# Weighing x by groups of row tiles in one-core attention with a feed-forward layer, with new orders on every engine

## The reference

```python
q = rope(x @ wq);  k = rope(x @ wk);  v = x @ wv          # one head of 128, float32
s = (q * 128 ** -0.5) @ (k * 128 ** -0.5).T
p = softmax(s - 1e30 * (column > row))                    # causal
x1 = layernorm(x + (p @ v) @ wo)
h = gelu(x1 @ binarized(w1).T + b1)                       # 128 -> 512
y = layernorm(x1 + h @ binarized(w2).T + b2)              # 512 -> 128
```

## Time and profile before

| | us |
|---|---|
| Median of three timed runs (lowest, highest) | 294.69 (294.51, 294.73) |
| The profiled execution | 292.43 |
| Its span in the profile | 290.6 |
| PE busy | 265.5 |
| PEld busy | 234.9 |
| ACT busy | 235.2 |
| DVE busy | 230.8 |
| POOL busy | 165.0 |

### The profile page before, as it was taken

One profiled execution on the slowest core, in us unless ns is written; L12 is line 12 of the kernel. 1 busy time (PEld: TensorE's weight loads), 2 busy tenths in 40 slices (PEclk: granted clock), 3 DMA queues, 4 the chain that ended last, 5 costly groups with the idle time before them and its releaser, 6 DMA issues.

```text
span 290.6 us, 5773 instructions
## 1 busy us (share of the span) xinstructions
PE 265.5 (91%) x1831; PEld 234.9 (81%) x1831; DVE 230.8 (79%) x581; ACT 235.2 (81%) x396; POOL 165.0 (57%) x250
## 2 busy tenths in 40 slices
PE   2779899999979999999999999999999999998760
PEld 2668798998968898889888998998898988896530
DVE  1589989999987996799779976999789457446883
ACT  3185776646599979998899999688999899898892
POOL 2150520561256595639981895269849968888223
PEclk9999999999999999999999999999999999999796
DMA  8951251258649627742586128702663230202205
GB/s 197 200 72 41 52 77 28 62 127 162 134 87 177 175 63 126 174 107 51 94 167 160 26 63 208 178 3 63 194 157 82 59 83 0 76 0 74 71 2 144
DMA packets 58013, 29.22 MB, mean 101 GB/s; under 512 B 33408, under 2 KB 54400, under 8 KB 57984
## 3 DMA queue, kind: packets, MB, share of 16 engines
q1 hardware_dynamic: 57168, 28.07, 43.2%
q10 hardware_dynamic: 816, 0.79, 0.8%
HBM read 9.18 MB, written 4.19 MB: 46 GB/s over the span
## 4 chain that ended last, share of the span: by engine, by line
PE 76%; ACT 10%; DVE 6%; issue 4%; POOL 2%; DMA 2%; SPq 0%; ACTq 0%; POOLq 0%; DVEq 0%
PE bank L561 21%; PE pair L537 16%; PE bank L572 5%; PE bank L621 5%; PE bank L622 5%; PE bank L613 4%; PE pair L590 3%; PE pair L591 3%; PE pair L603 2%; PE pair L605 2%; PE pair L604 2%; PE bank L579 2%; DMA hid<-in_L_attn_wk_dram 2%; ACT hid L987 2%; PE bank L658 2%
## 5 line engine op out<-in xcount | busy, mean ns | idle before, releaser
L359 POOL TENSOR_TENSOR hid_lo<-hid,hid_hi 128x1024 fp32r<-128x1024 f32 x28 | 66.4, 2386 | 25.8 <-ACT hid_hi L994 25.7
L561 PE MATMUL bank<-probT,xa 128*128 128x128 f32 x576 | 69.3, 276 | 0.0
L561 PEld LDWEIGHTS bank<-probT,xa 128*128 128x128 f32 x576 | 66.8, 192 | 0.5
L948 ACT ACTIVATE prob<-pair,negmax 128x128 f32<-128x128 f32 (+3 forms) x64 | 47.4, 741 | 10.6 <-DVE negmax L1399 8.9
L1399 DVE TENSOR_REDUCE negmax<-pair 128x1 f32<-128x128 f32 (+3 forms) x64 | 47.2, 746 | 8.9 <-PE pair L540 8.8
L324 POOL TENSOR_TENSOR tok<-rot_cos,rot_sin 128x512 f32<-128x512 f32 x16 | 20.5, 1281 | 39.4 <-ACT tok L963 39.3
L1409 DVE STREAM_TRANSPOSE turned<-prob 128x128 f32<-128x128 f32 (+7 forms) x56 | 39.1, 719 | 0.0
L537 PE MATMUL pair<-qkT_hi 128*128 128x512 f32 (+2 forms) x96 | 37.5, 391 | 0.3 <-ACT hid L987 0.2
L537 PE MATMUL pair<-qkT_hi,qkT_lo 128*128 128x512 f32 (+2 forms) x96 | 33.3, 347 | 0.0
L537 PE MATMUL pair<-qkT_lo,qkT_hi 128*128 128x512 f32 (+2 forms) x96 | 33.1, 345 | 0.0
L987 ACT ACTIVATE hid<-pair,b_sb,alpha 128x1024 f32<-128x1024 f32 x28 | 33.0, 1208 | 0.1
(11 more groups left out here) (111 smaller groups left out, 638.4 us busy)
## 6 DMA issues: line engine op xcount, KB each, us to landing
probT<-turned SPq DMA_DIRECT2D x96, 104.0 KB, 2.2
probT<-turned SPq DMA_DIRECT2D x128, 40.0 KB, 1.9
xq<-in_L_attn_x_dram SPq DMA_DIRECT2D x28, 128.0 KB, 3.8
xa<-in_L_attn_x_dram SPq DMA_DIRECT2D x7, 512.0 KB, 3.9
out_dram<-res SPq DMA_DIRECT2D x7, 512.0 KB, 3.6
hid<-in_L_ffn_w_dram SPq DMA_DIRECT2D x2, 256.0 KB, 2.9
out_dram<-res SPq DMA_DIRECT2D x2, 256.0 KB, 2.3
xa<-in_L_attn_x_dram ACTq DMA_DIRECT2D x1, 256.0 KB, 3.6
```

The lines of the kernel that those rows point to most:

```text
L359: pool.tensor_tensor(hid_lo[:, j, :], hid[:, j, :], hid_hi[:, j, :].bitcast(F32), ALU.subtract).then_inc(s_hid_lo[j], 1)
L561: ins = pe.matmul(bank_of["px", r // TG, c][:, me], xa[c % 2][:, j, :], probT[g][:, :, spot + j, :], start=j == 0, stop=j == r)
L948: act.activation(prob[r % 3][:, 0:(r + 1) * P], pair_of["score", r, c][:, 0:(r + 1) * P], ACT.Exp, bias=negmax[:, r:r + 1], accum_out=rows ...
```

## The change

Three things are changed.

First, the squares of a group are laid out by column tile j and not by row: square j of row r stands at 4 j + (last row - r). So the squares of all rows of a group with the same j are neighbours, and one product takes up to four of them, 512 columns, with x's tile j as weights. For j beyond the first row of the group only the later rows take part, and the product has 384, 256 or 128 columns. `weigh_group(g, first, last, c)` computes tiles first to last of a group; group 1 is called in two pieces. Group 1 of images 0 and 7 goes on row by row (`weigh_row`). The layout leaves gaps, so a group has 13 and 29 squares, which the carry moves too; POOL sets the gaps to zero at the start. The result's rows stand in reversed order in the bank, and `project_out` reads them so.

Second, score row 4 (640 columns) begins at column 192 of its pair of banks, so it is cut in 320 and 320 columns and not in 512 and 128.

Third, the order of the calls is new on every engine. `x1T_high` on ACT gets a wait for `up` of the image before, since a transpose of x1 can now be issued ahead of an `up`.

The core of the diff; of the orders it shows two lines, and the pieces behind it show the rest.

```diff
-    SPOT = {r: (g, r * (r + 1) // 2 - rows[0] * (rows[0] + 1) // 2) for g, rows in enumerate(GROUPS) for r in rows}
-    SQUARES = [sum(r + 1 for r in rows) for rows in GROUPS]
+    SPOT = {r: (g, rows[-1] - r) for g, rows in enumerate(GROUPS) for r in rows}
+    SQUARES = [TG * rows[-1] + 1 for rows in GROUPS]
...
+        def squares(r, first, last):
+            return slice(SPOT[r][1] + TG * first, SPOT[r][1] + TG * last + 1, TG)
+        def columns(r):
+            first = BANK - (r + 1) * P // 2 if r == TG else 0
+            return first, first + (r + 1) * P
...
             def carry(g, c):
+                if by_squares(GROUPS[g][-1], c) == 1:
+                    sp.wait_ge(s_const, 7 + 4)
                 sp.wait_ge(s_turned[GROUPS[g][-1]], by_squares(GROUPS[g][-1], c))
...
+            for g, rows in enumerate(GROUPS):
+                for j in rows[1:-1]:
+                    pool.memset(turned[g][:, :, TG * j + rows[-1] - j + 1:TG * (j + 1), :], 0.0).then_inc(s_const, 1)
...
-                for lo in range(0, (r + 1) * P, BANK):
-                    hi = min(lo + BANK, (r + 1) * P)
-                    diagonal = hi == (r + 1) * P
+                first, last = columns(r)
+                for lo, hi in ((first, min(last, BANK)), (BANK, last)):
+                    if lo >= hi:
+                        continue
+                    diagonal = hi == last
                     for n, (qp, kp) in enumerate(parts):
-                        ins = pe.matmul(dst[:, lo:hi], qp[:, 0, me], kp[:, 1, lo:hi],
+                        ins = pe.matmul(dst[:, lo:hi], qp[:, 0, me], kp[:, 1, lo - first:hi - first],
                                         start=n == 0, stop=n == 2 and not diagonal)
...
-            def weigh(r, c):
...
+            def weigh_group(g, first, last, c):
+                rows = GROUPS[g]
+                if first == 0:
...
+                    pe.wait_ge(s_probT_in[g], carried(g, c))
+                    next_bank("px", g, c)
+                for j in range(first, last + 1):
+                    n = rows[-1] - max(j, rows[0]) + 1
+                    ins = pe.matmul(bank_of["px", g, c][:, 0:n * P], xa[c % 2][:, j, :],
+                                    probT[g][:, :, TG * j:TG * j + n, :].rearrange("p n m i -> p m n i"),
+                                    start=j == 0, stop=j == rows[-1])
+                if last == rows[-1]:
+                    ins.then_inc(s_px[last], 1)
...
             def x1T_high(h, c):
                 act.wait_ge(s_x1T[h], c + 1)
+                if c > 0:
+                    act.wait_ge(s_up[NF - 1], c)
...
-                scores(7, b - 1)
...
-                weigh(4, b - 3)
+            weigh_group(1, 0, 3, 2)
+            scores(7, 3)
```

More of the change, by code:

```diff
@@ L926, in _ @@
-            opening()
-            for b in range(5, 7):
-                step(b)
-            ending()
+            turn_x0(0)
+            turn_x0(1)
+            project(0, 0)
+            project(1, 0)
+            turn_qk(0, 0)
+            turn_qk(1, 0)
+            turn_qk(2, 0)
+            setup_turn_wv()
+            scores(0, 0)
+            scores(1, 0)
+            scores(2, 0)
+            scores(3, 0)
+            setup_wvo()
+            turn_qk(3, 0)
+            project(0, 1)
@@ new lines, in _ @@
+            project(1, 1)
+            scores(4, 0)
+            scores(5, 0)
+            scores(6, 0)
+            scores(7, 0)
+            turn_row(4, 0)
+            setup_turn_sgn1()
+            setup_turn_sgn2()
+            project(0, 2)
+            turn_row(5, 0)
+            turn_qk(0, 1)
+            turn_qk(1, 1)
+            project(1, 2)
+            weigh_group(0, 0, 3, 0)
+            turn_qk(2, 1)
+            scores(0, 1)
+            turn_qk(3, 1)
+            turn_row(6, 0)
@@ new lines, in _ @@
+            project_out(0, 0)
+            turn_row(7, 0)
+            scores(1, 1)
+            turn_qk(0, 2)
+            scores(2, 1)
+            scores(3, 1)
+            scores(4, 1)
+            scores(5, 1)
+            scores(6, 1)
+            scores(7, 1)
+            weigh_row(4, 0)
+            weigh_row(5, 0)
+            turn_qk(1, 2)
+            weigh_row(6, 0)
+            weigh_row(7, 0)
+            scores(0, 2)
+            scores(1, 2)
+            scores(2, 2)
+            project_out(1, 0)
@@ new lines, in _ @@
+            scores(3, 2)
+            project(0, 3)
+            turn_qk(2, 2)
+            turn_qk(3, 2)
+            project(1, 3)
+            weigh_group(0, 0, 3, 1)
+            turn_x1(0, 0)
+            scores(4, 2)
+            project_out(0, 1)
+            scores(5, 2)
+            scores(6, 2)
+            turn_x1(1, 0)
+            scores(7, 2)
+            weigh_group(1, 0, 3, 1)
+            turn_qk(0, 3)
+            weigh_group(1, 4, 7, 1)
+            up(0, 0)
+            project_out(1, 1)
@@ L947, in exponentials @@
                         act.wait_ge(s_turned[last[0]], by_squares(*last))
-                act.activation(prob[r % 3][:, 0:(r + 1) * P], pair_of["score", r, c][:, 0:(r + 1) * P], ACT.Exp,
+                act.activation(prob[r % 3][:, 0:(r + 1) * P], pair_of["score", r, c][:, slice(*columns(r))], ACT.Exp,
                                bias=negmax[:, r:r + 1], accum_out=rowsum[:, r:r + 1]).then_inc(s_exp[r], 1)
@@ L1146, in _ @@
+            qkT_high(2, B - 4)
+            qkT_high(3, B - 4)
+            gelu(1, 1)
+            gelu(2, 1)
+            gelu(3, 1)
+            exponentials(0, B - 4)
+            pxT_copy(0, 3)
+            exponentials(1, B - 4)
+            hidden_high(0, 1)
+            x1T_high(0, 2)
+            exponentials(2, B - 4)
+            xT_high(1, B - 3)
             exponentials(3, B - 4)
+            exponentials(4, B - 4)
+            exponentials(5, B - 4)
             hidden_high(1, 1)
-            exponentials(4, B - 4)
```

1207 lines of the change are left out of this document (559 added, 648 removed).

## The result

| | us |
|---|---|
| Changed kernel, median (lowest, highest) of 6 runs | 292.04 (291.92, 292.28) |
| Kernel before on the same chip, median (lowest, highest) of 6 | 294.6 (294.18, 295.59) |
| Ratio, 95% interval | 0.9915 (0.9898 to 0.9932) |
| Profiled execution after, its span | 291.92, 290.1 |

The change takes 2.6 us (0.85%) off the median, and 4.7 were forecast.

A forecast was written before the change was run, and what follows sets the result against it. PE was taken as the bound (busy 265.5 of 290.6 us, full over 180 us in the middle). Terms -1.9 - 0.8 - 2.0 = -4.7 us took the median from 294.7 to 290.0; 80% range 285.5 to 296.5.

The forecast's parts named there:

- Weighing x, -1.9: Weighing on PE: 236 products of 128 columns become 80 wide f32 ones, saving 1.9 us.
- The rivals of one pass (0.23): Weighing: wide f32 streams once, records 0.23 us apart, 25.3 us leave PE, 278 in all; chance 0.04.
- float32r's pace (0.46): Weighing: wide f32 runs at float32r's pace in both passes, 2.1 us lost, 294.0 in all; chance 0.08.
- Score row 4, -0.8: Score row 4 in 320 and 320 columns instead of 512 and 128, in 8 images, saves 0.8 us.
- The table loads and the stall, -2.0: At 80 to 100, two ACT table loads go and PE's waits with them; 2.0 us saved, bounds 0 and 2.4.
- A carry comes late: Weighing in images 2 to 6 waits for the carry's DMAs, 298; late carries or a like new wait: chance 0.20.
- the term 928/832: Carry issue of 11.23 us stretched by 928/832 columns if held up by data, taking 1.3 us more.
- The opening and the end keep their chains. I take 0 for both: The new order's opening and end cost 0, with 1 us either way.
- The order gives back nothing but the edits count: Only weighing and score row 4 gain: -2.7 us, 292.0; inside the likeliest range, no chance of its own.
- Lay it on the median: The difference worked out against the 292.43 us profiled execution is applied to the median, 2.3 us above.
- The period of an image, 0.35 shorter: Sign in the middle: the period between weighed groups about 0.35 us shorter than 30.96.

The follow-up runs named there:

- e3: The kernel before with only score row 4 cut in 320 and 320 columns; 293.48 us, ratio 0.9963.
- e6: The changed kernel with score row 4 back in 512 and 128 columns, wide weighing and new orders kept; 292.9 us, ratio 0.9949.
- e2: The changed kernel's orders and layout, but single products of 128 columns and score row 4 in 512 and 128; 296.0 us, ratio 1.0055.
- e7: The changed kernel with weighing in single products of 128 columns, score row 4 in 320 and 320 and new orders kept; 294.56 us, ratio 1.0007.
- e11: The changed kernel with a one-element exponential between the Gelus of image 0, bringing back two ACT table loads; 296.07 us, ratio 1.0032.
- e9: The changed kernel with 20 useless identity products keeping PE busy in the opening; 289.63 us, ratio 0.9824.
- e10: The kernel before with useless identity products keeping PE busy in the opening; 291.27 us, ratio 0.9884.
- e4: The changed kernel with every engine's order as in the kernel before up to the weighing of image 0; 296.3 us, ratio 1.0052.
- e5: The changed kernel with DVE's feed-forward weight signs moved behind score row 6 and PE's projection of image 2 ahead of their transposes; 292.11 us, ratio 0.9919.
- e1: The new layout, wide weighing and 320 and 320 columns in the orders of the kernel before; 296.2 us, ratio 1.0048.
- e12: The changed kernel with both the useless identity products in the opening and the feed-forward weight signs later; 289.56 us, ratio 0.9834.

## Why the prediction was right, and where its size was off

- **Weighing x, -1.9: right.** The records stand 0.429 us apart where 0.43 was forecast. 76, 28, 28 and 28 of them at 0.429, 0.322, 0.215 and 0.111 are 50.8 us, for 472 at 0.1117 of before, 52.7: 1.9 less. The rivals of one pass (0.23) and of float32r's pace (0.46) are out.
- **Score row 4, -0.8: right.** 0.8 by the records, 1.3 measured alone (e3), 0.9 to 1.5 in the new orders (e6, and e2 against e7).
- **The table loads and the stall, -2.0: right.** 80 to 100 lost 0.8 for 3.0, and e11 brought the stall back with two loads. How the 2.2 divide between the loads and the other moves in that stretch is not shown.
- **A carry comes late: did not occur.** The room for image 2 is 1.1 us, where I had worked out that it would be 1.1 late. The carry began at 86.99 as before (87.02) and was no slower (10.94 for 11.23), so the wider DMAs are not issued more slowly; the term 928/832 was wrong. The group was weighed at 100.73, 1.5 us earlier than before and not 3.4 to 3.8. The prediction had let the projection behind row 7 fall away; in the new order half a projection (12 records, 98.80 to 100.30, 1.5 us) that stood at 87.73 before is ahead of the group, and PE ends row 6 0.4 later (98.80 for 98.39).
- **"The opening and the end keep their chains. I take 0 for both": this is the step that failed.** It is why the gain is 2.6 and not 4.7. I had seen that the orders change there and priced it at 0 with 1 us either way. Against e3, which opens as the kernel before does, the changed kernel loses the same from 0 to 20 and 2.3 us more from 20 to 40: the 1.18 at 27.88, the 1.88 at 34.07, and a clock of 0.64 and 0.50 at 34 to 38, where e3 had 1.00. (e3's clock fell for longer at 16 to 23 than the changed kernel's at 17 to 21, which makes the 2.3 a low figure; e9 against e10 gives 3.1. Both lie outside the 1 us that was allowed.) That eats the 2.2 of the stall, and the edits' 2.5 are left. This is a sum over profiled executions. No run won the loss back: e4 and e5 took parts of it away, and other waits came in their place. *The order gives back nothing but the edits count*, at 292.0, is the case that came true, though by a gain and a loss that cancel and not by nothing happening. The changed kernel's rows of the table of stretches:

```profile
18.00:20.00 2.00, 2.00 (x12) 1.91 (x11) 1.14 (x3) 0.60 (x1) 1.82 (x2) 0.50 0.01 1
...
34.00:36.00 2.00, 1.93 (x12) 1.96 (x13) 2.00 (x3) 1.97 (x3) 0.00 (x0) 0.64 0.34 85
36.00:38.00 2.00, 2.00 (x11) 2.00 (x11) 1.81 (x7) 1.28 (x4) 0.65 (x1) 0.50 0.21 52
```

- **"Lay it on the median": right, but for a reason that the text did not have.** The profiled execution of before was of a rarer kind. Of the 67 timed executions of the kernel before that ran beside the experiments, five had a mean clock of 0.985 and took 292.6 to 293.2; the 62 others, at 0.979 or less, took 293.8 to 295.6. Its profile (clock 0.986, 292.43) seems to lack some 2 us that PE usually loses in the opening: e3's, at the clock of the many (0.977), loses 1.9 more from 0 to 40. No usual execution of the kernel before itself was profiled. Who compares the two profiled executions finds 0.5 us of gain; the medians tell the 2.6.
- **The period of an image, 0.35 shorter: a bad test.** The wide group stands at another place of each image, and from image 2 on the intervals between its starts run from 28.9 to 31.8. The executed work tells it.

What stays open: why the edits in the old orders (e1) lose over 3 us at 180 to 240 in three separate waits, for ACT, for DVE and one without a releaser, rather than in one place; whether the opening's loss can be won back in the new orders; and what the loss at the end (e12) has to do with the removal of the one at 34 to 38.

## What to carry to other kernels

An order written out by hand and the lengths of the tasks in it belong together: here either half alone cost 1.2 to 1.4 us and both together gained 2.6, though score row 4 alone gained 1.3 in the old orders. So price the opening of a new order wait by wait and not at 0. Before a difference is laid on one profiled execution, hold its mean clock against that of the timed runs. Where TensorE waits a microsecond or two at the start, products that nobody needs may pay: 20 of them gave 2.4 us here, almost as much as the whole change, and 289.6 is the best time of all.

## What the runs showed of the hardware

A plain float32 record of up to 512 columns costs in proportion to its columns (0.111, 0.215, 0.322, 0.429 us), so wide moving operands save almost nothing per column; what they save is about 6 ns for each of the 312 records that go (4 x 0.1117 against 0.429). PE's first records come at half pace (256 columns 0.21 us apart until 12 to 13 us into the span) while the profile's clock column reads 1.00; with fillers from 2.33 on the records stood 0.11 (128 columns) or 0.12 (256) apart from 6 to 8 us on. And a wait of 1 to 2 us in the opening, behind the loads of e11 or near the end was often, not always, followed by 2 to 7 us at a granted clock of 0.50 (the 1.2 GHz level). In e3 the clock was at 0.50 for 6 us after waits of 2.04 and 0.65, in the profile of before it stayed at 1.00 after 1.75 and 1.07 at the same places, and so it did in the changed kernel after the 1.18 at 27.88.
